# Attention's first sequence prepared in the drain of a pipeline, and the values product moved to the end of each pipeline step

## What is computed

```python
# stack (DEPTH = 2 layers, 8 heads of 64, window 64), run before and after the attention
h = shift_token(x); q, k, v = split(h @ wqkv, 3)
q, k = l2norm(q) * qs, l2norm(k) * ks; q, k = rotary_xpos(q, k)
o = softmax(mask(8 * q @ k.T in windows of 64 and the one before)) @ v
x = x + o @ wo
h = shift_token(x); h = (h - mean) / sqrt(var + 1e-5) * lg + lb; h = h @ w1 + b1
a, g = split(h, 2); x = x + (a * gelu(g)) @ w2 + b2
# attention (s = a sequence)
values, k, q = (layernorm(y @ W + b) * g + beta for each of v, k, q)
out = softmax(k @ q.T) @ values + y
```

## Time and profile before

| | us |
|---|---|
| median of 3 runs | 1849.92 (1849.67 to 1853.71) |
| the profiled execution's own time | 1851.99 |
| its span in the profile | 1850.2 |
| TensorE matmul busy | 1532.3 (83%) |
| TensorE weight loads busy | 1241.0 (67%) |
| VectorE busy | 1326.1 (72%) |
| ACT busy | 1176.9 (64%) |
| GpSimd busy | 1099.0 (59%) |

### The profile page before, as it was taken

One profiled execution on the slowest core, in us unless ns is written; L12 is line 12 of the kernel. 1 busy time (PEld: TensorE's weight loads), 2 busy tenths in 40 slices (PEclk: granted clock), 3 DMA queues, 4 the chain that ended last, 5 costly groups with the idle time before them and its releaser, 6 DMA issues.

```text
span 1850.2 us, 44040 instructions
## 1 busy us (share of the span) xinstructions
PE 1532.3 (83%) x15864; PEld 1241.0 (67%) x15864; DVE 1326.1 (72%) x3419; ACT 1176.9 (64%) x2460; POOL 1099.0 (59%) x1130
## 2 busy tenths in 40 slices
PE   1789999978899999655788978899998899999984
PEld 1577777767777777532566657777776677777763
DVE  6687979776879787523445358887877778878773
ACT  1576767665767676514655747776766667767671
POOL 3685858574868585403323257766756667768560
PEclk9999999999999999865989899999999999999997
DMA  8241222222222121040000042121223121212113
GB/s 277 47 124 43 52 50 58 57 81 62 59 50 52 46 52 42 20 140 23 24 23 12 23 110 51 43 56 39 64 50 94 45 73 42 56 42 60 46 28 115
DMA packets 183670, 112.46 MB, mean 61 GB/s; under 512 B 86720, under 2 KB 164128, under 8 KB 182944
## 3 DMA queue, kind: packets, MB, share of 16 engines
q1 hardware_dynamic: 183456, 109.65, 22.7%
HBM read 43.41 MB, written 23.42 MB: 36 GB/s over the span
## 4 chain that ended last, share of the span: by engine, by line
PE 51%; DVE 24%; ACT 11%; issue 6%; SPq 3%; DMA 3%; POOL 2%; DVEq 0%; ACTq 0%; POOLq 0%
PE QK L372 9%; PE TO L613 8%; PE TO L680 5%; PE QK L613 5%; DVE rope_c L1018 5%; DVE rope_s L1023 4%; DVE o_n L1043 4%; DVE top L962 3%; PE TO L372 3%; PE SC L654 3%; DVE h2n L1030 3%; ACT probs L1180 3%; PE TO L780 2%; PE VB L780 2%; PE TO L726 2%
## 5 line engine op out<-in xcount | busy, mean ns | idle before, releaser
L1180 ACT ACTIVATE probs<-SC,shift,qgain 128x128 f32<-128x128 f32 x1024 | 390.7, 481 | 103.4 <-DVE shift L970 103.3
L1347 POOL TENSOR_TENSOR ve<-mv,epsilon 128x1 f32<-128x1 f32 x128 | 24.5, 192 | 404.1 <-DVE mv L1009 404.1
L372 PE MATMUL QK<-w_qkv,hT 128*128 128x512 f32 x768 | 220.3, 423 | 20.0 <-DMA w_qkv<-qkv_d 10.9
L1018 DVE TENSOR_TENSOR rope_c<-QK,rope 128x512 f32<-128x512 f32 x256 | 175.5, 686 | 77.1 <-PE QK L372 74.4
L1360 POOL TENSOR_TENSOR rnorm<-clip,mhalf 128x8 f32<-128x8 f32 x128 | 211.1, 1649 | 12.1 <-DVE clip L979 12.0
L1369 POOL TENSOR_TENSOR qgain<-clip,mhalf 128x8 f32<-128x8 f32 x128 | 209.5, 1637 | 0.0
L613 PE MATMUL TO<-ident,probs 128*128 128x128 f32 x1280 | 191.5, 277 | 18.7 <-ACT probs L1180 10.1
L962 DVE TENSOR_REDUCE top<-SC 128x4 f32<-128x512 f32 x256 | 174.6, 682 | 28.8 <-PE SC L654 28.6
L1174 ACT ACTIVATE v_own<-VB 128x512 f32<-128x512 f32 x128 | 76.5, 598 | 182.7 <-PE VB L372 182.7
L1023 DVE TENSOR_TENSOR rope_s<-QK,rope 128x256 f32<-128x256 f32 x512 | 190.5, 413 | 0.0
L613 PEld LDWEIGHTS TO<-ident,probs 128*128 128x128 f32 x1280 | 154.9, 143 | 52.3 <-issue 32.9
(11 more groups left out here) (147 smaller groups left out, 3775.6 us busy)
## 6 DMA issues: line engine op xcount, KB each, us to landing
v_prev<-v_own SPq DMA_DIRECT2D x256, 130.0 KB, 2.3
x_att<-stream SPq DMA_DIRECT2D x128, 64.0 KB, 2.2
h<-stream SPq DMA_DIRECT2D x256, 32.0 KB, 1.9
stream<-x_new SPq DMA_DIRECT2D x32, 256.0 KB
w_qkv<-qkv_d SPq DMA_DIRECT2D x3, 1536.0 KB, 7.4
h<-x_mid SPq DMA_DIRECT2D x128, 32.0 KB
h<-x_mid SPq DMA_DIRECT2D x128, 31.8 KB
rope<-rope_d SPq DMA_DIRECT2D x24, 128.0 KB, 3.2
```

The costliest lines, as they stand in the source:

```text
L372: last = mm(dst, fr(left(a)), fr(right(b)), start=(k == 0), stop=(k == 2))
L1018: v.tensor_tensor(qk(rope_c[:])[:, m], src, rope[:, i, m, 0:1, :].to_broadcast([P, HEADS, DH]), ALU.mult)
L1180: last = nc.scalar.activation(probs[:, b, hd, :], SC[:, hd * P:hd * P + P], ACT.Exp, bias=shift[:, b, hd:hd + 1], scale=qgain[:, b, hd % 4 ...
```

## The change

It has two parts.

1. *Preparation of sequence 0 in the drain.* `prepared` now answers only for sequences 1 to 3. The pieces of sequence 0 are issued from a hook `after(g)` that `pipeline` calls after every step, in steps 65 to 71 of the first stack (`DRAIN` = 66), and inside VectorE's last burst. They use other buffers (x_2b, pT2, v_own's columns as z_0, v_prev's as x_h1) and the PSUM banks SC and QK. The loop over g starts at -1. The stores of the first stack are waited for only by SP and by ACT's first `out_normalised`. In the attention loop the joined input moves ahead of the row's maximum, y's normalise ahead of the copy pT, z's first normalise behind the exponentials. The last `out_normalised` and SP's part with it move from step 1 and 2 to step 3 of the second stack.
2. *The values product at the end of the step.* On TensorE it moves from behind Q and K to behind the transposes of h and h2n, on ACT the copy v_own to behind hT and h2T. The transposes of h and h2n go to TT instead of VB. The first half of the probabilities' transposes and the burst's first product wait for the low parts; VectorE makes the low parts ahead of the norm sum.

The diff, cut to its core:

```diff
-        if g == 1 and after_two:
-            after_two()
+        if after:
+            after(g)
+DRAIN = NT + QKV
@@ prepared
-    return s if r == 0 and 0 <= s < SEQS else None
+    return s if r == 0 and 1 <= s < SEQS else None
@@ SP
-                for n in range(SEQS + 1, ITERS):
+                for n in range(SEQS + 1, ITERS - 1):
                     iteration(n)
+                def half_step_loads():
+                    sp.dma_start(x_2b[:], rows(x_in[0])).then_inc(g_ld, 16)
+                    sp.dma_start(v_g[:], rows(stream[DEPTH, 0, 1:, :])).then_inc(g_ld, 16)
+                iteration(ITERS - 1, () if k else [(0, half_step_loads)])
...
+                if k == 0:
+                    sp.dma_start(x_att[:], rows(x_in[1])).then_inc(g_ld, 16)
+                    sp.wait_ge(s_o, NT)
+                    sp.dma_start(x_h1, rows(stream[DEPTH, 1, 1:, :])).then_inc(g_ld, 16)
@@ TensorE, step
                     if t := tile(ATT):
+                        if t2 := tile(TH + 1):
+                            pe.wait_ge(s_hl, t2.count())
+                        if t2 := tile(FFN_IN + 1):
+                            pe.wait_ge(s_h2l, t2.count())
                         probs_transposed(t, 0)
...
-                        product(mm, VB[:], lambda x: hT[:, b, x, :], lambda x: w_qkv[:, x, 1024:1536]).then_inc(s_v, 1)
...
-                        transpose(VB[:, 0:P], h[:, t.i % 4, :]).then_inc(s_th, 1)
+                        transpose(TT[:, 0:P], h[:, t.i % 4, :]).then_inc(s_th, 1)
...
-                        transpose(VB[:, P:2 * P], h2n[:, t.i % 2, :]).then_inc(s_th2, 1)
+                        transpose(TT[:, P:2 * P], h2n[:, t.i % 2, :]).then_inc(s_th2, 1)
+                    if t := tile(QKV):
+                        b = t.i % 2
+                        need(pe, s_vown, t.count(back=1))
+                        if before is not None:
+                            pe.wait_ge(s_xn, before * 2 + 1)
+                        product(mm, VB[:], lambda x: hT[:, b, x, :], lambda x: w_qkv[:, x, 1024:1536]).then_inc(s_v, 1)
@@ TensorE, w1_pair
+                    if k == 0:
+                        pe.wait_ge(s_h2l, last_in.count())
+                        if t := tile(TH):
+                            pe.wait_ge(s_hl, t.count())
+                    if k == 1 and n == ITERS - 1:
+                        pe.wait_ge(g_z, TILES)
@@ TensorE, after(g)
+                if g == DRAIN + 2:
+                    pe.wait_ge(g_yn, 1)
+                    pe.wait_ge(s_p, NT * 2)
+                    for half in range(2):
+                        for i in range(HALF):
+                            last = transpose(SC[:, half * 512 + i * P:half * 512 + i * P + P], pT2[:, half * HALF + i, :])
+                        last.then_inc(g_ty, 1)
+                if g == DRAIN + 3:
+                    for i in range(TILES):
+                        if i < 4:
+                            pe.wait_ge(g_yT, 2)
+                        else:
+                            pe.wait_ge(g_z, i - 3)
+                        dst = QK if i % 4 >= 2 else SC
+                        mm(dst[:, i % 2 * 512:i % 2 * 512 + 384], y_T[:, i * P:i * P + P],
+                           w_kqv[:, :, :].rearrange("p a b -> p (a b)"), start=True, stop=True).then_inc(g_pr, 1)
+                if g == DRAIN + 5:
+                    for m, dst in ((0, SC), (1, QK)):
+                        pe.wait_ge(g_zn, m + 1)
...
@@ VectorE, after(g) and step
+                if g == DRAIN - 1:
+                    joined(0)
+                if g == DRAIN:
+                    joined_stats(0, range(HALF))
+                if g == DRAIN + 1:
+                    joined_moments(0, joined_stats(0, range(HALF, TILES)))
+                if g == DRAIN + 3:
+                    for i in range(4):
+                        shifted_in(0, i)
+                if g == DRAIN + 4:
+                    z_stats(0, TILES - 1)
+                    z_moments(0)
...
-                if t := tile(QKV):
-                    b = t.i % 2
-                    dve.wait_ge(s_sq, t.count())
...
                 if t := tile(TH):
...
                 if t := tile(FFN_IN):
...
+                if t := tile(QKV):
+                    b = t.i % 2
+                    dve.wait_ge(s_sq, t.count())
...
+                if burst == ITERS - 1:
+                    for i in range(4, TILES):
+                        shifted_in(0, i)
+                    z_stats(0, 0)
                 if burst is not None:
                     for k in range(6):
+                        if n == ITERS - 1:
+                            z_stats(0, k + 1)
@@ ACT, step
                 if t := tile(ATT):
                     exponentials(t, 1)
-                if t := tile(QKV):
-                    b = t.i % 2
-                    act.wait_ge(s_v, t.count())
...
                 if t := tile(FFN_IN):
                     act.wait_ge(s_th2, t.count())
-                    copy(fr(h2T[:, 0, t.i * P:t.i * P + P]), VB[:, P:2 * P]).then_inc(s_h2T, 1)
+                    copy(fr(h2T[:, 0, t.i * P:t.i * P + P]), TT[:, P:2 * P]).then_inc(s_h2T, 1)
+                if t := tile(QKV):
+                    b = t.i % 2
+                    act.wait_ge(s_v, t.count())
...
@@ ACT, after(g)
+                if g == DRAIN + 2:
+                    y_normalised(0)
+                    y_moved(0, 0)
+                    y_moved(0, 1)
+                if g == DRAIN + 4:
+                    z_normalised(0, 0)
+                    z_normalised(0, 1)
+                if g == DRAIN + 5:
+                    for m in range(2):
+                        z_moved(0, m, 0)
+                        z_moved(0, m, 1)
+                    z_normalised(0, 2)
@@ GpSimd, after(g)
+                if g == DRAIN + 1:
+                    rstd_and_shift(LN_IN, 1, g_mvi, g_rsi, g_nbi)
+                if g == DRAIN + 2:
+                    pool.wait_ge(g_yn, 1)
+                    residual(0)
+                if g == DRAIN + 4:
+                    for m in range(3):
+                        rstd_and_shift(KQV + m * TILES, m + 1, g_mvk, g_rsk, g_nbk)
```

More of the change, by code:

```diff
@@ L74, in need, with pipeline @@
         eng.wait_ge(sem, count)
-def pipeline(step, stack, after_two=None):
+def pipeline(step, stack, after=None):
     def tile_of(g):
@@ L820, in z_turned, with after @@
                 last.then_inc(g_tk, 1)
-            for g in range(-AHEAD, ROWS + 2):
+            def after(g):
+                if g == DRAIN + 2:
[17 more added lines that the diff above has]
+                        pe.wait_ge(g_zn, m + 1)
+                        for half in range(2):
+                            for i in range(HALF):
+                                last = transpose(dst[:, half * 512 + i * P:half * 512 + i * P + P],
+                                                 z_0[:, half * HALF + i, m * DIM:m * DIM + DIM])
+                            last.then_inc(g_tk, 1)
+            pipeline(step(0), 0, after)
+            pe.wait_ge(s_xn, ITERS * 2)
+            for g in range(-1, ROWS + 2):
                 if t := row(g):
@@ new lines, in joined, with joined_stats @@
+            def joined(s):
+                dve.wait_ge(g_ld, s * 32 + 32)
+                need(dve, g_xy, s)
+                v.scalar_tensor_tensor(out=flat(x_m(s)), in0=(flat(v_g), x_h1.rearrange("p t c -> p (t c)"), flat(x_b2), flat(x_b2))[s], scalar=0.5, in1=flat(x_att if s else x_2b),
+                                       op0=ALU.mult, op1=ALU.add).then_inc(g_x1, 1)
+            def joined_stats(s, tiles):
+                dve.wait_ge(g_x1, s + 1)
+                for k in tiles:
+                    last = stats(x_m(s)[:, k, :], LN_IN + k)
+                return last
@@ L1247, in _ @@
             act.wait_ge(s_vone, 1)
-            pipeline(step, 0)
-            stack_done(act, 0)
             def normalise(dst, src, slot):
@@ L1278, in out_normalised, with y_normalised, after @@
                     act.wait_ge(g_new[s - 1], 16)
+                else:
+                    stack_done(act, 0)
                 normalise(x_new, x_o[s % 2], LN_OUT).then_inc(g_on, 1)
-            for g in range(-AHEAD, ROWS + 1):
+            def y_normalised(s):
+                act.wait_ge(g_nbi, s + 1)
+                if s >= 2:
+                    act.wait_ge(g_ty, s * 2)
+                    act.wait_ge(g_xy, s)
+                normalise(y_n(s), x_m(s), LN_IN).then_inc(g_yn, 1)
+            def after(g):
+                if g == DRAIN + 2:
[10 more added lines that the diff above has]
+                    z_normalised(0, 2)
+            pipeline(step, 0, after)
+            for g in range(-1, ROWS + 1):
                 if (s := prepared(g, 2)) is not None:
@@ L1317, in _, with after_attention @@
                     out_normalised(t[1])
-            pipeline(step, 1, lambda: out_normalised(SEQS - 1))
+            def after_attention(g):
+                if g == 3:
+                    out_normalised(SEQS - 1)
```

(2 more changed lines are left out.)

188 lines of the change are left out of this document (100 added, 88 removed).

## The result

The changed kernel takes 2209.9 us (median of 4 runs, 2202.2 to 2215.4) against 1849.8 us for the kernel before (4 runs, 1848.5 to 1853.7): a ratio of 1.194, 95% interval 1.190 to 1.198. The forecast was 1843 us. The profiled execution spans 2208.3 us against 1850.2.

| stretch | before | after | difference |
|---|---|---|---|
| 112 intervals without a burst, fill, drains and layer changes included | 1051.4 | 1414.3 | +362.9 |
| 14 intervals with a burst | 339.2 | 378.5 | +39.3 |
| the one with the drain's burst and the attention stage | 336.6 | 294.9 | -41.7 |
| ahead of the first o_n and behind the last | 123.1 | 120.6 | -2.4 |

What follows compares the result with a forecast made beforehand. Bounds: the seam's chain of single waits and the blocked step's chain through x_mid, GpSimd up to k_r, h2n, top and o_n. 1852.0 + 31.1 - 39.7 + 1.3 = 1844.7, less 2.1, about 1843 us; range 1806 to 1865.

Steps and rivals of the forecast that it cites:

- part 1: Feed-forward pipeline step with the values product moved: steps, bursts and second drain together cost +31.1 us.
- part 2: Seam between first pipeline and attention: sequence 0 prepared inside the drain, SP's loads costing 0; gain 39.7 us.
- Steps of 9.41 ... a fixed point: Full pipeline steps: x_mid at 3.86 leaves q_r at 0.46 again, so steps settle at 9.41 us, +0.22 or +0.30.
- The quick form is lost: VectorE's h2n in the step: at 7.34, behind k_r at 7.27 in every step, so no quick steps remain.
- Q behind the output product at 3.72: TensorE's Q product in the step: starts at 3.72 instead of 3.36, since qT ends at 3.68.
- The bursts: 14 intervals with a feed-forward burst: each 0.5 us later, 0.15 more for four ending in a quick step; 7.6 us.
- The seam: From first pipeline's end to attention's first score: 857.97 becomes 818.3, gain 39.7 us, bounds 30 and 44.
- eight projections of 0.82 us: TensorE in the drain: sequence 0's projections, behind tile 62's h2n transpose, end near 792.6.
- Rival 3: Pipeline step: the held shift feeds the new wait, delay 0.44, 94 steps lose 43 us; 1864 us, chance 0.15.
- Rival 2: Pipeline step: the new wait is hidden, steps keep 9.19 and 9.11; 1821 us, chance 0.12.
- rival 4: Seam: gives only 30 us, the y part standing ahead of the last output product; 1853 us, chance 0.08.
- Rival 1: Pipeline step: values product fills TensorE's gap, step shortens to 8.74, 41 us gained; 1780 us, chance 0.12.

Runs made afterwards that it cites:

- experiment 1: The changed kernel with SP's three h2 DMAs put ahead of the wait for v_own and its two v_prev DMAs: 1866.5 us.
- experiment 2: The kernel before with only the drain-time preparation of sequence 0 added, its old step kept: 1811.5 us, ratio 0.979.
- experiment 8: experiment 1 with rnorm moved ahead of ve, rstd and x_b on GpSimd: 1787.3 us, ratio 0.966.
- experiment 5: The kernel before, its v_prev DMAs also waiting on SP for ACT's h2T copy, with the h2 DMAs put ahead of that wait: 1863.9 us.
- experiment 4: The kernel before with one wait added on SP: the v_prev DMAs also wait for ACT's h2T copy: 2177.5 us, ratio 1.177.
- experiment 6: The changed kernel with values product and v_own copy back in mid-step, shared bank and SP's order kept: 1857.7 us, ratio 1.0041.

## Why the prediction was wrong, point by point

**The step that failed** is the costing of the moved v_own copy in part 1: "ACT's copy of the values, like oT's about 0.5 us, moves ahead of oT, kT and qT". It counted what the copy delays on ACT, not who waits for the copy. SP does, and has h2's DMAs queued behind. SP entered the prediction only with part 2's loads. What the runs showed in its place: the copy moved about 5 us later, SP's h2 DMAs went with it past a slack of 0.7 us, and the step became 12.54 us instead of 9.41. The trace before showed whom to ask: SP waited 513 us for v_own. The sum of the waits alone says nothing (606 us in experiment 1, without harm); the slack of 0.7 us says it, and it takes SP's rows and one pair of issue and statistics.

**"Steps of 9.41 ... a fixed point"** followed: the circle through SP was not among the chains looked at. With SP's order mended the step is 9.50 us (experiment 1), so without the missed queue the term is 0.31 instead of 0.22: the low parts end 2.30 us behind o_n, not 2.23, the transposes start at 2.40, and x_mid is at 3.95 instead of 3.86. "The quick form is lost" and "Q behind the output product at 3.72" hold there: h2n takes 1.11 us in the middle one (0.86 to 1.19), Q starts at 3.76. In the changed kernel itself h2n is quick (0.34), for the wrong reason: everything waits for the DMA.

**The bursts**, 7.6 us in the sum, came to 17 in experiment 1 against experiment 2. 0.5 a burst is right; missing was that behind the added wait of 0.99 us the granted clock fell in eight of fourteen, 1.2 us each. Rows of this were not in the trace before.

**The seam** is right, in one term by luck: 39.7 less 1.3 in the attention's loop against 39.4 measured in experiment 2. Counted from the last o_n of the first stack (773.75 before, 774.76 there), each time of the forecast came within 2.3 us, all a little early: last output product 7.38 us behind it (forecast 7.95), first act 21.78 (23.35), first score 42.28 (44.55). The gain up to the first score is 41.9 us, and the attention behind it lost 2.6 where 1.3 were forecast.

The luck is in the eight projections. The two matmuls of 1.65 us in the earlier trace rows are one projection, not two (the kernel before has 64 such matmuls for 32 projections), so "eight projections of 0.82 us" was half of what those rows say: 13 us, or 10.7 at the pace of the first two below, not 6.6. They took 6.5, since the clock came back, which the forecast had only as its upper bound. The first two and the next two projections, and the granted clock in both stretches (last but two of the numbers):

```profile
786.20 2.67 PE L862 MATMUL SC<-w_kqv,q_r 128*128 128x384 f32 x4
788.71 1.45 PE L862 MATMUL QK<-w_kqv,q_r 128*128 128x384 f32 x4
```

```profile
786.20:788.70 2.50, 2.50 (x5) 1.35 (x5) 0.85 (x2) 0.28 (x1) 0.00 (x0) 0.51 0.26 69
788.70:792.70 4.00, 4.00 (x14) 2.16 (x13) 2.52 (x6) 0.00 (x0) 1.16 (x3) 1.00 0.79 231
```

From the last act's start to the first score it is 13.8 us (forecast 818.3 less 804.45, the start of an act that ends at 805.2: 13.9), and in the changed kernel 13.8 too (993.71 to 1007.51):

```profile
993.71 0.75 DVE L1200 SCALAR_TENSOR_TENSOR act<-QK,b,gelu 85x512 f32<-85x512 f32 x1
```

```profile
1007.51 3.75 PE L886 MATMUL SC<-rope_s,rope_c 128*128 128x512 f32 x4 [0.96 <-ACT rope_s L1367]
```

**The rivals.** Rival 3 had the side, not the mechanism: the second shift is held 1.28 us in the changed kernel, but the same step with SP's order mended has it at 0.42. Rival 2 falls (9.50 us with the queue mended, not 9.19), and so does rival 4 (37 us, not 30). Rival 1 turned out to be what the order can do when GpSimd lets it (experiment 8). The part that adds up to 31 us in the forecast is 55 in experiment 1 against 2: about 32 in steps, 17 in bursts, 10 at fill and layer changes, where the late v_own holds the weights' loads in SP's list (experiment 5), less 4 ahead of the first o_n and 2 in the attention.

**Range and chances.** The range's upper end took in only delays of the chains already known. No case stood for a queue not looked at.

## What to carry to other kernels

When an instruction moves later, list everyone who waits for its semaphore, and for each of them everything queued behind that wait; a queue that only issues DMAs counts like an engine. For each transfer so delayed, compare issue plus the landing time with the first use, and take the slack from the trace: here 0.7 us under a move of 5. The Trainium skill (DMA: Bandwidth & Descriptors, "Anatomy of one DMA — SWDGE (gpsimd) path") says that a DMA's wait for a semaphore is spent on the issuing sequencer before dispatch; experiment 4 agrees, 328 us for a wait on transfers that nobody needed yet. Put the transfer that is due first at the head of the list.

## What the runs showed of the hardware

- A wait of 0.99 us on TensorE, behind one of 0.68 ahead of the o_n transposes, was followed by a granted clock of 0.72 over the next six us in eight of the twelve bursts of experiment 1 that have both waits. In experiment 6 (0.74 to 1.28 us, then 0.98 or more) it was eight of fourteen. Where the first wait was 0.04 us or less (two bursts of experiment 1, thirteen of experiment 8) the clock stayed at 1.00, even behind a single wait of 1.50 us. What decides between the bursts that have both stays open.
- From the issue of the last of three short transfers within SBUF to the instruction that waits for it: 2.95, 2.92 us. The issues themselves take 0.5 to 0.8 us each on SP, five of them 3.3 us: a third of a step of 9.19.
- Where GpSimd stood against VectorE went with the length of whole steps: the same shift took 0.16, 0.42, 0.96, 1.19 or 1.28 us, by where q_r or k_a stood.
